# A graph-network kernel: node rows and their split table computed inside the sort's scatter, the distance formula in four parts in the first gather pass, and the first one-hots in four buffers

## The reference

```python
h = jnp.maximum(_layernorm(x, axis=-1), 0.0)
x = x + _L0_gnn_ref(h, edge_index, L0_gnn_weight)

def _L0_gnn_ref(input, edge, weight):
    h = mobius_matvec(weight, input, C)
    dist = sqdist(h[edge[0]], h[edge[1]], C)[None, :]
    edge_h = C / (C + dist)
    h_e = logmap0(h, C)
    edge_h_e = logmap0(edge_h, C)[0]            # one norm over all edges
    edge_e = jnp.exp(-jax.nn.leaky_relu(edge_h_e, ALPHA))
    e_rowsum = jax.ops.segment_sum(edge_e, edge[0], num_segments=N)[:, None]
    h_prime = jax.ops.segment_sum(edge_e[:, None] * h_e[edge[1]], edge[0], num_segments=N)
    out = jax.nn.elu(h_prime / e_rowsum)
    return proj(expmap0(out, C), C)
```

## Time and profile before

| | |
|---|---|
| median of 3 runs | 18782.4 us (18748.1 to 19046.8) |
| the profiled execution | 18755.8 us, its span 18754.0 us |
| POOL, DVE, PE, ACT busy | 11223 us (60%), 7657 us (41%), 4881 us (26%), 2120 us (11%) |
| constants and node rows | 0 to 227.3 us |
| sort until the first scatter | 227.3 to 761.6 us |
| scatter | 761.6 to 4942.7 us |
| split table | 4942.7 to 4994.6 us |
| first gather pass | 4994.6 to 10101.9 us |
| distance formula and weights | 10101.9 to 10291.7 us |
| first sums | 10291.7 to 11247.0 us |
| second layer and end | 11247.0 to 18754.0 us |

### The profile page before, as it was taken

The page is one execution under the profiler, slowest core; times in us unless marked ns, Lnnn a source line. Parts: engine busy times, 40 slices in busy tenths (PEclk is TensorE's granted clock), DMA queues, the critical chain, the costliest instruction groups (busy, mean ns, idle before and its releaser), DMA issues. The chain is left out here.

```text
span 18754.0 us, 142433 instructions
## 1 busy us (share of the span) xinstructions
PE 4880.6 (26%) x28224; PEld 3611.6 (19%) x28225; DVE 7656.7 (41%) x14407; ACT 2119.6 (11%) x4439; POOL 11223.1 (60%) x12446
## 2 busy tenths in 40 slices
PE   0000000000011111111111882232323232328997
PEld 0000000000000000000000881111111111113996
DVE  5779600000133333333335884333333333336775
ACT  2000000000000000000000760000000000005333
POOL 0267777777666666666662772666666666650773
PEclk6555555555555555555555995566556556569998
DMA  2000000000122222222223441222222222257331
GB/s 51 3 4 5 5 5 5 5 5 5 35 73 73 71 73 72 72 73 73 73 73 37 140 136 35 65 69 64 67 65 67 66 66 67 66 71 234 106 106 59
DMA packets 770958, 1143.40 MB, mean 61 GB/s; under 512 B 322012, under 2 KB 469339, under 8 KB 770652
## 3 DMA queue, kind: packets, MB, share of 16 engines
q1 hardware_dynamic: 386972, 666.22, 11.7%
q0 software_dynamic: 322304, 245.26, 8.4%
q10 hardware_dynamic: 61632, 231.44, 3.1%
HBM read 872.56 MB, written 269.54 MB: 61 GB/s over the span
## 5 line engine op out<-in xcount | busy, mean ns | idle before, releaser
L1323 POOL DMA_INDIRECT big<-b_d,big x3424 | 3278.0, 957 | 2274.6 <-POOLq L140 1239.6
L854 POOL DMA_INDIRECT big<-h_d,big x3424 | 3270.4, 955 | 1832.2 <-issue 1100.1
L607 POOL DMA_INDIRECT rec_d<-big x3224 | 3099.3, 961 | 1608.1 <-issue 983.6
L889 PE MATMUL ps<-big 128*128 x3424 | 740.3, 373 | 8746.8 <-PEq L140 5220.7
L889 PEld LDWEIGHTS ps<-big 128*128 128x128 bf16 x3424 | 442.5, 162 | 9044.4 <-issue 9041.7
L908 DVE TENSOR_REDUCE ps<-ps 128x260 f32<-128x780 f32 x856 | 837.6, 978 | 3278.8 <-remote 1441.9
L1450 DVE TENSOR_REDUCE ps<-ps 128x256 f32<-128x768 f32 x856 | 827.6, 967 | 2541.0 <-DVEq L140 1383.9
L1649 POOL TENSOR_SCALAR big<-iota_f,big 128x128 f32<-128x128 f32 x1498 | 875.3, 604 | 842.5 <-DMA big<-rec_d 528.5
L1402 PE MATMUL ps<-big 128*128 x3424 | 610.0, 336 | 2752.9 <-issue 2286.3
L628 DVE CAST big<-big 128x896 f32 (+2 forms) x9 | 8.3, 918 | 2778.4 <-DMA big<-h_d 2777.4
L1402 PEld LDWEIGHTS ps<-big 128*128 128x128 bf16 x3424 | 444.7, 159 | 3112.4 <-issue 3112.3
(11 more groups left out here) (347 smaller groups left out, 9734.5 us busy)
## 6 DMA issues: line engine op xcount, KB each, us to landing
big<-e_d SPq DMA_DIRECT2D x428, 512.0 KB, 3.2
rows_d<-big ACTq DMA_DIRECT2D x214, 544.0 KB
big<-rows_d SPq DMA_DIRECT2D x214, 544.0 KB, 3.3
HA<-slots_d SPq DMA_DIRECT2D x214, 512.0 KB
big<-slots_d SPq DMA_DIRECT2D x214, 512.0 KB
e_d<-big ACTq DMA_DIRECT2D x214, 512.0 KB
big<-rec_d SPq DMA_DIRECT2D x860, 64.0 KB, 3.0
big<-h_d,big POOLq DMA_INDIRECT x3424
```

The source lines that it names most:

```text
L607: gp.indirect_dma_start(rec_d, bass.IndirectOffsetOnAxis(ix_stage[b][:, j:j + 1], 0), rec_stage[b][:, j * REC:(j + 1) * REC], None).then_i ...
L854: gp.indirect_dma_start(G[g][:, t * ROW:(t + 1) * ROW], None, h0_d, bass.IndirectOffsetOnAxis(idx[g % 2][:, t:t + 1], 0)).then_inc(gath[g] ...
L889: m = t.matmul(XS[q % 2][:, n, 0:3 * D + 3], OT3[g % 2][:, o, :], T0[:, ds(chunks[o // 2] * TW, 3 * D + 3)], start=True, stop=True)
L1323: gp.indirect_dma_start(G[g][:, t * D:(t + 1) * D], None, b_d, bass.IndirectOffsetOnAxis(idx[g % 2][:, t:t + 1], 0)).then_inc(gath[g], 16)
```

## The change

- Node rows (phase 2) and split table (phase 4) are no phases any more. DVE does both behind its last rank span, inside the sort's phase; PE's loop is there too, and the copy between its two products is made by DVE instead of ACT. ACT's nine functions for them stand between its staging loops, the first behind ten pieces, the others two pieces apart (`stage_pairs`). SP loads x behind the blank records, and stores the rows before it loads the attributes of piece 22. The load of the rows from `h0_d` is gone, and so is POOL's clearing of HA. src, dst, the counts and small arrays lie in HA.
- The distance formula is done in four parts of 1024, 1024, 768 and 608 columns. `each_block` is cut at blocks 64, 128 and 176, and behind each cut (and the end) DVE does the formula for the columns finished, and ACT the root and the logarithms for them.
- In the first sums the one-hots and the weights have four buffers instead of two. ACT waits for the products of block k - 4, and makes 5 tiles instead of 4; DVE makes 7 instead of 8.

```diff
             @block.scalar
...
-                with a.Fori(0, NRB // 2 - 1) as h:
-                    for ab in range(2):
-                        stage_block(h * 2 + ab, ab, h * 32 + 32)
+                def stage_pairs(h0, h1):
+                    with a.Fori(h0, h1) as h:
+                        for ab in range(2):
+                            stage_block(h * 2 + ab, ab, h * 32 + 32)
+                stage_pairs(0, 5)
+                a.wait_ge(n_v, 7)
+                a.activation(RT, VA, ACT.Sqrt).then_inc(n_a, 1)
+                stage_pairs(5, 6)
+                a.wait_ge(n_v, 20)
+                a.activation(XN, T1, ACT.Sqrt).then_inc(n_a, 1)
+                a.activation(MN, T2, ACT.Sqrt).then_inc(n_a, 1)
+                stage_pairs(6, 7)
...
                 for r in range(NRB):
                     if r >= 2:
                         sp.wait_ge(st_rdy[1], 4 * (UPR // 2) * (r - 1))
+                    if r == NRB - 4:
+                        sp.wait_ge(n_v, 82)
+                        sp.dma_start(h0_d.rearrange("(c p) w -> p c w", p=P), ROWS).then_inc(n_rows, 16)
...
+        PARTS = (0, 16, 32, 44, NBLK // 4)
...
+            for q in range(4):
+                with eng.Fori(PARTS[q], PARTS[q + 1]) as i:
+                    for g in range(4):
+                        body(g, i, i * 4 + g)
+                if q < 3 and part is not None:
+                    part(q)
...
+                def part_functions(q):
+                    c, n = part_columns(q)
+                    a.wait_ge(s_dist, q + 1)
+                    a.activation(W1[:, 0:n], R2[:, c], ACT.Sqrt).then_inc(s_root, 1)
+                    a.wait_ge(s_clip, q + 1)
+                    a.activation(W1[:, 0:n], R2[:, c], ACT.Ln, bias=1.0).then_inc(s_logs, 1)
+                    a.activation(W2[:, 0:n], R2[:, c], ACT.Ln, bias=1.0, scale=-1.0).then_inc(s_logs, 1)
+                each_block(a, store, part_functions)
...
+                def part_weights(q):
+                    c, n = part_columns(q)
+                    w1, w2, w3, w4, r = W1[:, 0:n], W2[:, 0:n], W3[:, 0:n], W4[:, 0:n], R2[:, c]
+                    link, done = chain(v, s_n, loop=True)
+                    distance_norm(v, link, XY[:, c], X2A[:, c], EDG3[:, c, 0], w1, w2, w3, w4, r)
+                    v.sem_inc(s_dist, 1)
+                    v.wait_ge(s_root, q + 1)
+                    refine(v, link, w1, r, w2)
+                    link(v.tensor_scalar(r, w1, CLIP, None, ALU.min))
+                    v.sem_inc(s_clip, 1)
+                    v.wait_ge(s_logs, q * 2 + 2)
+                    link(v.tensor_tensor(w1, w1, w2, ALU.subtract))
+                    link(v.tensor_tensor(w1, w1, w1, ALU.mult))
+                    link(v.tensor_scalar(w1, w1, 1.0, None, ALU.add))
+                    link(v.reciprocal(w1, w1))
+                    link(v.tensor_tensor(r, w1, EDG3[:, c, 2], ALU.mult))
+                    done()
                 onehot(0)
-                each_block(v, step)
+                each_block(v, step, part_weights)
...
-        u0.mm_start = 2
+        u0.mm_start = 4
...
-        POOL0, ACT0 = 4, 8
+        POOL0, ACT0 = 4, 9
...
                 def weights(g, i):
-                    b = g % 2
-                    hold(a, "a", u0.mm[b], i * 4 + (2 + g // 2 * 2))
+                    hold(a, "a", u0.mm[g % 2], i * 4 + (2 + g // 2 * 2))
```

More of the change, by code:

```diff
@@ L549, in _ @@
                     c0 += w
+                link, k = chain(v, n_v)
+                v.wait_ge(n_x, 32)
+                link(v.memset(ROWS, 0.0))
+                layernorm(v, link, XN, VA, TMP, HN3)
+                v.wait_ge(n_a, 1)
+                layernorm_end(v, link, VA, RT, T1, HN3)
+                assert k[0] == 14
+                link(v.tensor_tensor(TMP, HN3, HN3, ALU.mult))
+                link(v.tensor_reduce(T1, TMP, AX, ALU.add))
+                link(v.tensor_scalar(T1, T1, 1e-30, None, ALU.max))
@@ new lines, in _ @@
+                with v.Fori(0, NIT) as i:
+                    v.tensor_copy(stage, big[:, ds(i * (CPI * D), CPI * D)]).then_inc(g_in, 1)
+                    hold(v, "v", g_tr, i + 1)
+                    v.tensor_copy(hT, ps[:, 0:CPI * D]).then_inc(g_cp, 1)
+                    hold(v, "v", g_mm, i + 1)
+                    v.tensor_copy(MX[:, ds(i * (CPI * D), CPI * D)], ps[:, 1024:1024 + CPI * D]).then_inc(g_out, 1)
+                v.wait_ge(g_out, NIT)
+                link(v.tensor_tensor(TMP, M3, M3, ALU.mult))
@@ new lines, in _ @@
+                link(v.tensor_reduce(T2, TMP, AX, ALU.add))
+                link(v.tensor_scalar(T2, T2, 1e-30, None, ALU.max))
+                v.wait_ge(n_a, 3)
+                refine(v, link, XN, T1, RC)
+                refine(v, link, MN, T2, RC)
+                link(v.tensor_scalar(RT, XN, CLIP, None, ALU.min))
+                v.wait_ge(n_a, 5)
+                artanh_finish(v, link, RT, LP, LM, SE, T1, T2, AT)
+                assert k[0] == 44, k
+                link(v.reciprocal(RC, XN))
@@ L556, in _ @@
                 t.matmul(ps[:, 512:512 + NC], tri, cnt, start=True, stop=True).then_inc(s_mm, 1)
+                t.wait_ge(n_wd, 32)
+                with t.Fori(0, NIT) as i:
+                    hold(t, "t", g_in, i + 1)
+                    for q in range(NPAIR):
+                        m = t.transpose(ps[:, q * P:(q + 1) * P], stage[:, q * P:(q + 1) * P], ident[:, :])
+                    m.then_inc(g_tr, 1)
+                    hold(t, "t", g_cp, i + 1)
+                    for q in range(NPAIR):
+                        m = t.matmul(ps[:, 1024 + q * P:1024 + (q + 1) * P], hT[:, q * P:(q + 1) * P], wblk,
+                                     start=True, stop=True)
+                    m.then_inc(g_mm, 1)
             @block.scalar
@@ L734, in build @@
         end_phase()
[L735 to L760 removed]
+        top[0] = NC * TW // 2
         EDG = take(NT * 3)
```

373 lines of the change are left out of this document (148 added, 225 removed).

## The result

The changed kernel takes 18730.0 us (median of 20 runs) against 18768.1 us for the kernel before (20 runs): a ratio of 0.9981, 95% interval 0.9975 to 0.9987. It is 38 us faster where 328 us were forecast (18440 against the 18768 of these runs), and it lies outside the range. Its profiled execution has a span of 18735.4 us, 19 us less than before.

| stage | before | after | difference | forecast |
|---|---|---|---|---|
| start to first scatter | 761.7 | 543.8 | -218 | -217 |
| first scatter's start to last one's end | 4173.0 | 4430.5 | **+257** | +5 |
| last scatter's end to first gather | 63.2 | 29.6 | -34 | -52 |
| first gather to the last gather's start | 5038.5 | 5188.0 | +149 | +133 |
| from there to the norm's Square | 225.2 | 88.4 | -137 | -126 |

The account below looks back on a forecast made before the run. POOL's indirect DMAs were taken to bound the scatter, POOL and DVE's lag the first gather pass, DVE the first sums. From 18755.8 us, 217 + 52 - 5 - 7 + 58 = 315 saved gives 18440 us, range 18345 to 18500.

Parts of the forecast that it names:

- The front: Before the sort: with the node rows moved away, the sort starts at about 10.5 us, 217 us saved.
- The first sums: One DVE tile fewer per block: pitch 4.24 us instead of 4.46, some 58 us saved over 214 blocks.
- ACT with its five tiles: First sums: rival that ACT's fifth tile makes it the bound, the 58 us gone, 18498 us; chance 0.13.
- The formula: Distance formula in parts: 126 us saved before the norm, 133 us lost at three pass stops, net loss 7 us.
- a pass without slack: First gather pass: POOL lives on DVE's lag of four blocks; stops cost 52, 45 and 36 us.
- the rival of the cheap stops: First gather pass: DVE closes up while POOL stands, 15 us a stop, 88 us better, 18350 us; chance 0.22.
- DVE's lag: First gather pass: DVE ends a block 85 to 98 us after POOL began it; 90 us taken.
- the step that decided: Scatter: DVE's moved node-row and table work, 138 plus some 35 us, fits into 2759 us of idle time.
- a rival for DVE's port: Scatter: POOL is stopped by DVE's moved work, up to 168 us more, 18608 us; chance 0.06.
- the signs that I had named as speaking against me: POOL waits of 30 us, scatters over 1.3 us from 1970 on, or one-hots 4.4 us apart with DVE awaiting PE.
- The 5 us for DVE's long instructions: Scatter: cost of DVE's moved work beside POOL's scatters, 5 us; 173 us if POOL stood throughout.
- The end of the phase: Between scatter and first gather: the split table's own phase goes, 52 us saved.

Follow-up runs that it names:

- e9: The changed kernel itself, measured once more without an edit: 18715.3 us against 18733.0 for the kernel before in its job, ratio 0.9989.
- e10: The kernel before plus seven PE transposes with one semaphore increment behind the last rank span, nobody waiting: 18735.8 us against 18733.0, one run.
- e5: The changed kernel with POOL waiting at two places of the scatter until all scatters so far landed: 16662.1 us against 17020.9 for before, ratio 0.9788.
- e6: The kernel before plus seven PE transposes with one semaphore increment behind the last rank span, nobody waiting: 17029.4 us against 17020.9, one run.
- e13: The kernel before plus fourteen exchanges of DVE and PE behind the last rank span, nobody else waiting: 18977.4 us against 18708.7, one run.
- e3: The changed kernel with each long DVE instruction of node rows and table cut in 7 to 9: 18654.5 us against 18715.4 for before, ratio 0.9959.
- e4: The kernel before with the change of the first sums alone: 18675.4 us against 18715.4 for before, ratio 0.9974.

## Why the prediction was wrong

**Right.** The front: the sort's first instruction at 9.58 (10.5 forecast), the first scatter at 543.8 (545), no gap in front of piece 10, -218 us for -217. The first sums: one-hots 4.15 us apart on the mean (4.24), -59 us for -58, and ACT with its five tiles not the bound. The norm's Square came 35 us behind DVE's last instruction of the pass, as forecast. The formula: it came out at 149 - 137 = +12 us for +7. At the first gather behind each stop POOL had fallen back by 40, 60 and 58 us more against before (52, 45 and 36 forecast); 8 us came back by the end, so 149 in all for 133, partly because the errors have different signs; the waits on POOL were 50.6, 64.3 and 55.2 us where I had said about 68. The part in front of the norm saved 137 us instead of 126. In the third job e9's pass took 112 us more than e10's, so the price is not firm to better than some 40 us. The idea of a pass without slack, which pays each stop in full, holds only in the late state: in the second job the pass of e5 is 18.6 us longer than that of e6, 6 us a stop. POOL's waits for DVE in the two jobs say why (the pass is L854, now L848 and L858; the wait is L140), the changed kernel first, then e5:

```profile
L848 POOL DMA_INDIRECT big<-h_d,big x3424 | 3279.5, 958 | 1939.0 <-issue 1100.4 <-POOLq L140 838.6
```

```profile
L858 POOL DMA_INDIRECT big<-h_d,big x3424 | 3279.2, 958 | 1082.8 <-issue 989.5 <-POOLq L140 93.3
```

There the gathers nearly bound the pass themselves, and the rival of the cheap stops (15 us a stop) would have been the nearer one. What I had called DVE's lag was late increments of PE: the waits at line 908 above.

**Wrong, the step that decided.** "It is 138 us busy at most plus some 35 for the table, against 2759 us of idle time", with 5 us taken for what lies beside the scatters. I asked when DVE is free and whether ACT's functions are ready, and priced DVE's work by its port. I took the loop of PE and DVE as work that is moved, and never as fourteen exchanges beside a POOL that issues without a pause. Its price was 265 us in e13, where it stands alone. What the runs show in its place: from unit 45 on the scatter is 250 us longer than before's in the changed kernel, and 250 in e13. The forecast had a rival for DVE's port (up to 168 us), and none for this. Of the signs that I had named as speaking against me, one came true: scatters longer than 1.3 us from 1970 us on.

**Mis-sized beside it.** The 5 us for DVE's long instructions: some 64 us where they fall into no late state (units of e5 that are 11.3, 15.9, 6.7, 15.2, 8.8 and 6.1 us longer). The row that I took, a tensor_scalar of 0.75 us, cost 0.39 us; a tensor_tensor on two SBUF operands costs POOL nearly its whole 6.69 us. The trace of before had a row for it, beside the one of the earlier trace rows that ends the last rank span:

```profile
2181.49 1.84 DVE L547 TENSOR_TENSOR HA<-big 128x1612 int32<-128x1612 int32 x1
2181.87 2.28 POOL L607 DMA_INDIRECT rec_d<-big  x1 [0.30 <-issue]
```

A scatter takes 2.28 us instead of 0.96 beside a tensor_tensor of 1.84; I had read the DVE line and not looked at POOL's. The Trainium skill ("SBUF — State Buffer", section "Who interferes with whom"), which I had for an estimate of 20 to 30 us, has such an instruction contend with GpSimd's reads but, as it infers, not hold up its descriptors. The trace disagrees: 6.75 us for a scatter beside one. That tensor_reduce doesn't contend agrees (0.96 us). Whether cutting it in pieces of 1.09 us makes it cheap where there is no late state isn't shown: e3 had one.

**The end of the phase.** 52 us were forecast for the table, 34 came. In e5, without the late state, it is 63.2 - 11.0 = 52: the table's phase is gone. The 19 us that are missing in the changed kernel (29.6 against 11.0) are there only with the late state; e13 has 13 us more at this place than before (76.5 against 63.2).

**The rest.** 22 us in code that the change doesn't touch are what two executions differ by: in the first job e3 and e4 take the same time there within 7 us.

**The sum without the late state.** e5 is the changed kernel with two waits of 1.8 us. Against before in its job it is 359 us faster (16662 to 17021). So without the late state more than the 315 us of the sum came, but not term by term: the formula brought -108 us from the first gather to the norm (4450.4 against 4558.3 in e6) instead of +7, and the scatter cost 69 us instead of 5. That the total is near the sum is in part luck.

## What to carry to other kernels

Idle time of an engine is not yet a place for its work: count the exchanges between engines as well as their busy time, above all beside an engine that issues indirect DMAs one behind the other. Look in the profile of before for stretches in which an engine waits for an increment of its own or of a neighbour that was long done ("remote", or an issue of many microseconds); if one is there, work with handshakes moved beside it can cost more than it hides. If it must go there, let the issuing engine stand for it: with 57 us of standing in it the scatter was still some 93 us shorter here, and a large store did less harm at the scatter's end. Look, too, at the neighbour's row beside each kind of instruction that is to be moved, and not at one kind alone.

## What the runs showed of the hardware

- Beside scatters 1.26 us apart, increments of some instructions came up to 35 us late. Those seen late are of instructions that write PSUM (PE's products, DVE's scan), while PE followed DVE's copy into SBUF within 0.2 us (2208.27 in the changed kernel), and scatters were seen landed 2 us behind the last one. The Trainium skill ("Perfetto Trace Analysis", section "Per-engine timelines") has TensorE push its increment when PSUM has acknowledged all bytes; no run here shows whether it is the acknowledgement or the increment that is late.
- The late state outlives its cause. Begun by 14 exchanges of 40 us or by a store of 3.4 MB, it lasted to the end of the scatter, 3010 us in e13. The stops of 51 to 95 us at the second rank span ended it; a hold of 10 to 15 us gave three units of 39.1 us and no more, a wait of 2 us nothing. The long units come five to seven units behind its start.
- The jobs with and without it differ by some 1700 us in the kernel before: 18.7 ms in four jobs, 17.0 in two, of which the two gather passes are 707 (5038.5 against 4331.5 us) and 939. PE and DVE exchange in every group of these passes, and in the first one DVE's waits for PE's products sum to 3234 us against 255. For the second pass the late state as the cause is argued, not shown.
- A scatter issued beside a DVE tensor_tensor on two SBUF operands took 6.75 us beside one of 6.69 us and 2.28 beside one of 1.84, instead of 0.96; beside a tensor_reduce of 6.69 us it took 0.96.
- A reciprocal of 608 columns took 3.95 us, a tensor_tensor on them 0.79 us.
